# A two-layer graph network: in the first query chunk the copy of the values moves from ScalarE to VectorE, and two pairs of activations become two activations

## What is computed

```python
# layer 0: masked attention of 8 heads (HEAD_DIM 16), then an MLP
qkv = layer_norm(x, g1, be1) @ w_qkv
scores = einsum('nhd,mhd->hnm', q, k) * SCALE
scores = where(adj != 0, scores, -inf)
x = x + (softmax(scores) @ v) @ w_proj + b_proj
x = x + gelu(layer_norm(x, g2, be2) @ w1 + b1) @ w2 + b2
# layer 1: one score per neighbour, weighted mean of the neighbours, layer norm
h = x @ Wt.T + bt
s = leaky_relu(h @ Wa.T + ba, 0.2)
w = softmax(where(adj > 0, s, NEG), axis=1)
y = x + (w @ h) @ Wp.T + bp
out = layer norm of y
```

## Time and profile before

| | |
|---|---|
| median of 3 runs | 1257.9 us (1256.56 to 1260.17) |
| profiled execution | 1256.3 us, span 1254.6 us |
| busy, share of the span | TensorE 93%, VectorE 90%, ScalarE 84%, GpSimd 77% |
| granted TensorE clock, mean | 0.988 of full speed |
| first chunk (steps 0 to 63) | from 19.5 us to about 192 us |
| chunks 1 to 7 | to about 1033 us, then the tail |

### The profile page before, as it was taken

One profiled execution on the slowest core, in us unless ns is written; L12 is line 12 of the kernel. 1 busy time (PEld: TensorE's weight loads), 2 busy tenths in 40 slices (PEclk: granted clock), 3 DMA queues, 4 the chain that ended last, 5 costly groups with the idle time before them and its releaser, 6 DMA issues. The chain is left out here.

```text
span 1254.6 us, 31457 instructions
## 1 busy us (share of the span) xinstructions
PE 1166.0 (93%) x11628; PEld 331.0 (26%) x11639; DVE 1124.4 (90%) x1622; ACT 1060.0 (84%) x1218; POOL 967.1 (77%) x1010
## 2 busy tenths in 40 slices
PE   5888899999999999999999899999999988999896
PEld 2222221111111111111112111111111114875443
DVE  6988889999999999999999899999999983664886
ACT  5999999999999999999999899999999992443000
POOL 5677679999999999999998788888888863454322
PEclk9999999999999999999999999999999997999998
DMA  4333336555544555455545444545455437513991
GB/s 163 107 120 93 119 85 190 158 151 149 182 137 135 153 159 145 136 168 161 155 142 170 135 136 135 169 138 145 140 180 150 127 92 294 211 60 118 361 400 30
DMA packets 52671, 194.40 MB, mean 155 GB/s; under 512 B 6496, under 2 KB 20640, under 8 KB 42272
## 3 DMA queue, kind: packets, MB, share of 16 engines
q1 hardware_dynamic: 38944, 156.65, 35.1%
q0 software_dynamic: 9216, 33.56, 13.1%
q10 hardware_dynamic: 4352, 2.10, 0.6%
HBM read 114.69 MB, written 44.04 MB: 127 GB/s over the span
## 5 line engine op out<-in xcount | busy, mean ns | idle before, releaser
L1403 DVE SCALAR_TENSOR_TENSOR probs<-m,ps 128x512 f32<-128x512 bf16 (+1 forms) x1024 | 926.4, 950 | 32.6 <-PE ps L1594 16.4
L1296 ACT ACTIVATE probs<-probs 128x1536 f32<-128x1536 f32 x512 | 849.1, 1659 | 0.9
L1185 POOL TENSOR_TENSOR probs<-probs,m 128x512 f32<-128x512 f32 x512 | 621.4, 1224 | 130.8 <-ACT probs L1290 98.3
L1609 PE MATMUL ps<-probs,v_sb 128*17 128x512 f32 x4096 | 540.3, 600 | 0.0
L1594 PE MATMUL ps<-kq 32*128 32x512 bf16 x6144 | 424.0, 378 | 54.8 <-DVE probs L1403 22.2
L1290 ACT ACTIVATE probs<-ps 128x512 f32<-128x512 f32 x512 | 392.4, 766 | 9.3 <-PE ps L1594 8.3
L1594 PEld LDWEIGHTS ps<-kq 32*128 32x128 bf16 x6144 | 116.6, 92 | 568.2 <-ACT probs L1290 430.0
L1178 POOL TENSOR_SCALAR m<-adj_in 128x512 bf16<-128x512 int32 x256 | 180.9, 707 | 0.3
L1609 PEld LDWEIGHTS ps<-probs,v_sb 128*17 128x17 f32 x4096 | 68.2, 95 | 217.8 <-issue 208.3
L455 ACT ACTIVATE probs<-ps 128x512 f32<-128x512 f32 x8 | 4.8, 597 | 75.2 <-PE ps L800 73.2
L811 PE MATMUL ps<-kq,probs 128*128 128x512 bf16 x245 | 57.7, 386 | 0.8 <-issue 0.2
(11 more groups left out here) (146 smaller groups left out, 627.1 us busy)
## 6 DMA issues: line engine op xcount, KB each, us to landing
adj_in<-in_adj_t SPq DMA_DIRECT2D x64, 1024.0 KB, 5.9
mask_t<-m SPq DMA_DIRECT2D x64, 512.0 KB, 2.9
counts<-m POOLq DMA_DIRECT2D x64, 512.0 KB, 4.6
kq<-mask_t SPq DMA_DIRECT2D x16, 2048.0 KB, 9.7
counts_t<-counts SPq DMA_DIRECT2D x8, 512.0 KB, 7.5
attn_t<-acc_sb SPq DMA_DIRECT2D x16, 256.0 KB, 6.6
adj_in<-attn_t SPq DMA_DIRECT2D x8, 512.0 KB, 3.9
q_shift<-in_x SPq DMA_DIRECT2D x8, 256.0 KB, 5.9
```

Source lines behind the costliest of these rows:

```text
L1185: nc.gpsimd.tensor_tensor(pr, pr, m01[:, (k // 2) % MRING, :], ALU.mult).then_inc(postmasked, 1)
L1296: nc.scalar.activation(pr, pr, ACT.Exp, scale=UNIT).then_inc(exped, 1)
L1403: nc.vector.scalar_tensor_tensor(out=pr, in0=m.to_broadcast([P, n, CH]), scalar=1.0, in1=ps[:, b:b + n, :], op0=ALU.subtract, op1=ALU.add)\
L1609: last = nc.tensor.matmul(ps[RT * hh:RT * hh + VW, 6 + g, :], v_sb[:, t, h * VW:(h + 1) * VW], probs[:, k % SLOTS, hh // 2, (hh % 2) * CH: ...
```

## The change

The values are copied by VectorE, ahead of both masks of step 8w+1 (behind the statistics, which stand at the end of step 8w), instead of by ScalarE ahead of its exponential of that step. `key_middle` and `query_middle` each make both head groups in one activation of 1024 columns, which waits for both rests and raises its semaphore by two; this holds for the prologue too.

```diff
@@ scalar
             def key_middle(j):
                 at = slice(j * CH, j * CH + CH)
-                for g in range(2):
-                    act.wait_ge(k_rest_made, 2 * j + g + 1)
-                    nc.scalar.activation(k_pack[:, g, 0, at], rest_k[:, g, :], ACT.Copy).then_inc(k_mid_made, 1)
+                act.wait_ge(k_rest_made, 2 * j + 2)
+                nc.scalar.activation(k_pack[:, :, 0, at], rest_k[:, :, :], ACT.Copy).then_inc(k_mid_made, 2)

             def query_middle(j):
                 at = slice(j * CH, j * CH + CH)
-                for g in range(2):
-                    act.wait_ge(q_rest_made, 2 * j + g + 1)
-                    nc.scalar.activation(q_pack[:, g, 1, at], rest_q[:, g, :], ACT.Copy).then_inc(q_mid_made, 1)
-
-            def values(j):
-                act.wait_ge(v_done, j + 1)
-                nc.scalar.activation(
-                    v_sb[:, j * SUB:(j + 1) * SUB, :].rearrange("p s (h k) -> p s h k", k=VW)[:, :, :, 0:HD],
-                    ps[:, pair_bank(PREP * j, 1), :].rearrange("p (s h k) -> p s h k", s=SUB, h=H), ACT.Copy)\
-                    .then_inc(v_made, 1)
+                act.wait_ge(q_rest_made, 2 * j + 2)
+                nc.scalar.activation(q_pack[:, :, 1, at], rest_q[:, :, :], ACT.Copy).then_inc(q_mid_made, 2)
...
-                if w < NC and o == 1:
-                    if w + 1 < NC:
-                        norm_turned(w + 1)
-                    values(w)
+                if w + 1 < NC and o == 1:
+                    norm_turned(w + 1)
@@ vector
+            def values(j):
+                dve.wait_ge(v_done, j + 1)
+                nc.vector.tensor_copy(
+                    v_sb[:, j * SUB:(j + 1) * SUB, :].rearrange("p s (h k) -> p s h k", k=VW)[:, :, :, 0:HD],
+                    ps[:, pair_bank(PREP * j, 1), :].rearrange("p (s h k) -> p s h k", s=SUB, h=H)).then_inc(v_made, 1)
...
             for k in range(TLS):
+                w, o = k // PREP, k % PREP
+                if w < NC and o == 1:
+                    values(w)
                 masks(k, 0)
-                w, o = k // PREP, k % PREP
                 if w + 2 < NC and o == 0:
                     statistics(w + 2)
```

## The result

| | before | changed |
|---|---|---|
| median (range) | 1257.67 us (1255.55 to 1260.17), 20 runs | 1260.33 us (1257.26 to 1261.67, without the one below), 20 runs |
| ratio | | 1.0018, 95% interval 1.0012 to 1.0025 |
| profiled execution: span | 1254.6 us | 1258.6 us |

A forecast was written before the change was run, and what follows sets the result against it. ScalarE was taken to bound the steady part, with the limit alternating inside the first chunk's windows. Terms +0.80 (prologue and window 0), +2.55 and -1.14 sum to +2.2 us: 1260.1 us, range 1254.0 to 1262.0.

The forecast's parts named there:

- Windows 1 to 5, the port: Steps 8w to 8w+7, first query chunk: GpSimd's low part blocks a tiny VectorE tensor-scalar; +0.51 us each, +2.55.
- the upper bound: Windows 1 to 5: of bounds -0.51 and +0.51 us a window, the loss was taken for all five.
- The free port rival: Windows 1 to 5: VectorE keeps winning the tie with GpSimd, gaining 0.51 us each; -2.9 in all, 1255.0; chance 0.25.
- Windows 6 and 7: No statistics there, the copy fits VectorE's idle time; ScalarE's 0.57 us is gained whole, twice: -1.14.
- Middle parts: On ScalarE, one activation of 1024 columns takes 0.95 us instead of 1.04 for two; 0.09 saved, key half gains nothing.
- The prologue: Before the first scores: the first query low part waits for both merged halves; +0.34 us, bounds 0 and 0.43.
- Window 0: Steps 0 to 7: VectorE's 0.60 us copy delays the masks, less 0.14 of waiting; +0.46 us.
- ScalarE as the only bound: Whole kernel: all ScalarE time saved counts, 8 x 0.48 + 14 x 0.09 = 5.1 us, 1252.8; chance 0.10.
- the dear copy: VectorE's copy writing with holes needs a second pass, 0.60 us more in windows 0 to 5; +5.8, 1263.7; chance 0.10.

The follow-up runs named there:

- the two halves alone: Kernel before with only the values moved to VectorE: ratio 0.9979; kernel before with only the middle parts merged: ratio 0.9991.
- without the tensor-scalars: Changed kernel, blocks 2 to 7: VectorE's two tiny tensor-scalars replaced by a tensor-reduce and epsilon on GpSimd; 1255.62 us, ratio 0.9982 against before.
- with both tensor-scalars kept: Changed kernel with GpSimd's two query low parts moved two steps and one step later; 1255.01 us, ratio 0.9976 against the kernel before.

## Why the prediction was right

- **Windows 1 to 5, the port** (forecast +2.55): right in mechanism, somewhat large. All five were blocked, against one before (two in its second profile), by GpSimd's low part moved ahead by the merged query half, and both were needed, as the two halves alone show. Measured +2.19, 0.44 a window for 0.51: VectorE lost 0.99 instead of the 1.02, and its mask led the scores by 0.82 (94.48 to 95.30) where I had used the exponential's 0.85. The reason for taking the upper bound held: GpSimd's low part, 0.06 behind the first tensor-scalar before, was to come ahead of it with an advance of 0.09, and it stood 0.01 to 0.03 ahead.
- **The free port rival** was what would have happened without the merge (-2.41) or without the tensor-scalars (-2.90); my 2.55 lies between. With the block gone the windows give more than 0.51: 0.56 with both tensor-scalars kept, since the mask leads the scores by 0.82 and not 0.85 there, and 0.58 without them, since VectorE, one tiny instruction shorter, is no longer later than ScalarE.
- **Windows 6 and 7** (-1.14): measured -1.14.
- **Middle parts**: 1047 ns, 0.95 start to start (89.97 to 90.92) as taken. The key half gains nothing: with the middle parts alone, windows 1 to 5 give 0.44, five times 0.09, one half and not two.
- **The prologue** (+0.34): the start of block 0's middle parts and of the first scores with the middle parts merged (ScalarE, TensorE):

```profile
15.58 1.05 ACT L1270 ACTIVATE kq<-tail_words 128x1024 bf16<-128x1024 f32 x1
16.56 1.06 ACT L1275 ACTIVATE kq<-acc_sb 128x1024 bf16<-128x1024 f32 x1
...
19.23 0.94 PE L1592 MATMUL ps<-kq 32*128 32x512 bf16 x12 [4.18 <-POOL kq L1133]
```

From the query middle part to the first scores 2.67 (16.56 to 19.23), before 2.33 (17.13 to 19.46): +0.34, where the forecast has 0.43 (1.05 less 0.62). The key half ahead of it takes 0.98 for 1.04 and gives back 0.06, where the forecast has 0.09. So it is +0.28 in all for the +0.34, and the start's clock scatters over it.
- **Window 0** (+0.46): depends on the clock. Where TensorE is slow the scores of step 1 are late anyway, and in the changed kernel's profile the masks and exponential of step 1 start together. Where it is not, as in the second profile of the values alone (VectorE, ScalarE):

```profile
23.55 0.68 DVE L1388 COPY v_sb<-ps 128x512 f32<-128x512 f32 x1
24.15 2.40 DVE L1400 SCALAR_TENSOR_TENSOR probs<-m,ps 128x512 f32<-128x512 bf16 x3
...
23.86 0.60 ACT L1283 ACTIVATE probs<-ps 128x512 f32<-128x512 f32 x1 [2.11 <-PE ps L1593]
```

the first mask starts 0.29 behind the exponential, with which it started before (both at 24.02). The term was 0 to 0.3 where these profiles let it be read, not 0.46.
- **The sum.** From step 8 to 58 the profile has +1.05 for a forecast of +1.41; the start is forecast at +0.80. The measured 2.3 would leave 1.2 for the start, but its interval (1.5 to 3.1) leaves 0.5 to 2.1. In the profiles the start looks dearer than forecast: the seven with block 0's values on VectorE reach step 8 at 0.80 to 2.84 (mean 2.11), the seven with them on ScalarE at 0 to 1.16 (mean 0.47), 1.6 apart for a forecast of 0.80. The times of the kernels do not show this, and whether the change makes it is open, as said above. The mechanism of the windows was right; that the sum comes out within 0.1 us of the forecast is in part luck: the windows' term was 0.36 too large, and the start, which no run fixes to better than a microsecond, made up for it. The rivals with ScalarE as the only bound (-5.1) and with the dear copy were both wrong: ScalarE was 4 us less busy and the kernel no faster, and the copy with its holes took 678 ns.

The Trainium skill, SBUF — State Buffer, section Who interferes with whom, has the exclusive lock between tensor-scalars in a two-port mode and GpSimd, and says that `tensor_reduce` never contends on trn2: the trace agrees with both, 1.17 us for the one and 0.16 for the other at the same place. It also says that whichever issues first blocks the other; the starts agree at 0.01 to 0.03 in the kernels with merged middle parts and not in window 3 before, where 0.02 was a tie.

## What to carry to other kernels

Work taken off the fullest engine is worth only what the next waiter leaves; go through the stage from wait to wait and ask which chain ends last behind the edit. Look at stalls that cost nothing: a lost tie of 1 us hidden behind another engine becomes a loss when that engine's work moves away, and advancing some third engine by 0.1 us can decide who wins. And keep tiny tensor-scalars of VectorE off the critical path where GpSimd works beside them, by another form of the instruction or by another time.

## What was not expected of the hardware

A tensor-scalar of four columns, 0.17 us alone, waits for the end of the GpSimd instruction that it meets: 1.17 us behind one that has just begun, and in window 0 of the kernel before 0.50, to the end of the mask product (tensor-scalar 23.38 to 23.88, GpSimd 22.70 to 23.85). A copy of 512 columns out of PSUM, beside a GpSimd that was busy 15.52 of 22 us, varies by 15 ns over its eight places. In these first 35 us TensorE's clock is granted at 0.50 in one to two spells of some 3 to 7 us, at different times in two profiles of one program, worth over a microsecond; windows 1 to 7 repeat to hundredths. Of two profiles that differ at the start, only what is compared from a common step on says something of the change.
